# Moving the final products, a transposition and a copy inside a block of 32 passes

## The chip, the cores and the metric

One core of a Trainium2 chip runs the whole kernel in one launch. The metric is the device time of the launch in microseconds, the median of its runs. The work of this case lies on five engines of that core: TensorE (PE, the matrix products and transpositions), VectorE (DVE), ScalarE (ACT, the activation functions), GpSimd (POOL) and SyncE (SP, which issues the DMAs).

## What is computed

The input `x` (16 batches of 256 rows of 256) first passes a gated cross part (a long convolution over a context, two small networks) and then a gated mixture of experts; only the second half matters here. With `h = layernorm(x) @ Wm + bm` split into 8 heads of 32, so that there are 4096 x 8 small vectors `t`:

```python
logits = t @ expert_emb                       # 16 experts
w = softmax(logits); topw, topi = top_k(w, 2)
hmid = gelu(einsum('td,edi->tei', t, W1) + b1)    # every expert, 32 -> 128
eo = einsum('tei,eio->teo', hmid, W2) + b2        # 128 -> 32
comb = (eo at topi * topw).sum(over the two)
out = comb.reshape(rows, 256) @ Wo + bo
x = x + tanh(g_ffn) * out
```

The kernel computes all 16 experts for every vector and multiplies by a weight that is zero for the experts that were not chosen.

## The kernel before, in words

The 4096 rows are 8 blocks of 512 rows (b = 0 to 7). The first third of the launch (to about 303 us) is the cross part. Then comes the expert loop: `n` from 0 to 256, one pass for each of 8 blocks x 2 groups of four heads (g) x 16 experts (e), so a block is 32 passes. "Pass 5" below means n % 32 == 5. Every engine walks the same loop in its own program, and semaphores tie them.

- TensorE (lines 844 to 865), in each pass: `up(2n+2)` (line 780, eight fp16 products, 512 wide, each on a strip of 32 columns of the array), `down(n-1)` (line 792, four fp32 products, eight in the records), then `up(2n+3)`, eight products again. `up(k)` writes one of three pairs of PSUM banks (`pre`: PT, and two in PA) and so waits for the gelu three before it. `down` writes one of the two banks of PB in turn.
- ScalarE: `gelu(2n+2)`, `gelu(2n+3)` (line 1582), each 128 x 1024, out of the pair that `up` filled. At pass 26 of block 0 it computes three exponentials (line 1474), with a table load before and after.
- VectorE: `down(n-1)` (line 1333) multiplies the result by its weights and adds the bias, which frees the PB bank; then one of 14 steps of `route` (lines 1142 to 1183), which chooses the two experts of the next block, at the passes listed in `ROUTE`.
- GpSimd (line 1677) adds each product to the sum `AC[g]` of its 16 experts.
- After the 16th expert, VectorE's `down` ends with a copy of the sum to fp16 (line 1340, the high part; it waits for GpSimd's last addition), and GpSimd subtracts it from the sum for the low part (line 1681).
- Final products of a block, `finish` (line 814 on TensorE, 24 products in fp16, 256 wide; line 1376 on VectorE): one for each quarter of the block (t = 0 to 3), in the block that follows, at the passes in `FIN`, at the end of the pass. They too take a PB bank, and VectorE frees it.
- The turn of weights, `weights_turned` (line 692: four fp32 transpositions of 128 x 128; line 1368 on VectorE copies them out): once a block, for the next block, at the passes in `WT_AT`, ahead of the first `up` of the pass. SyncE stores the result in DRAM (`keep_weights`, line 447) and loads it back spread out (`spread_weights`, line 458: four DMAs for every two passes, four places `WB` in turn); `store` (line 463) writes results out.

PB's two banks go round over all uses in the order of TensorE's program (`output_uses`), turns, logits, `down` and final products alike: a use waits until VectorE has emptied the use two before it.

Of the kernel before, what the change touches and what calls it, by code (L numbers as in the profile page):

```python
# [13 lines left out]
NB = 8  # L14
# [11 lines left out]
N = 256  # L26
# [15 lines left out]
ROUTE = (1, 2, 3, 5, 6, 8, 9, 11, 13, 14, 15, 17, 19, 21)  # L42
ROUTE1 = (10, 11, 12, 13, 14, 15, 16, 17, 18, 19, 20, 21, 22, 23)

FIN = (4, 10, 22, 28)

WT_AT = {32 * b - 7: b for b in range(1, NB)}
LG_AT, EXP_AT = {8: 5, 12: 6, 24: 7}, 26

ROUTE0 = {4: range(0, 4), 5: range(4, 5), 6: range(5, 10), 7: range(10, 14)}  # L50
# [48 lines left out]
    return out  # L99


def output_uses():

    out = []
    for n in range(N + 1):
        if n in WT_AT:
            out.append(("wt", WT_AT[n]))
        if n in LG_AT:
            out.append(("lg", LG_AT[n]))
        if n >= 1:  # L110
            out.append(("down", n - 1))
        if n >= 32 and n % 32 in FIN:
            out.append(("fin", 4 * (n // 32 - 1) + FIN.index(n % 32)))
    return out


def flamingo_kernel(nc, xd, ctxT, peT, wp1, wp2, win, w1a, w1b, w2a, w2b, wm, wo,
                    ew1, ew2, eb, cols, rows, ident, ramp, tvec, ones, out):
    with ExitStack() as ctx:
# [4 lines left out]
        def sem(name):  # L124
            return ctx.enter_context(nc.semaphore(name))
# [63 lines left out]
        AC = [WK[:, 2048 + 512 * i:2048 + 512 * i + 512] for i in range(2)]  # L189
# [55 lines left out]
        def combined(b, g):  # L245

            return WM if b % 2 and not g else {h: CM[h][:, 512 * g:512 * g + 512] for h in "hl"}

        def iteration(n):
            return n // 32, n // 16 % 2, n % 16  # L250
# [17 lines left out]
        p_up, p_down, p_fin = (sem("p_" + n) for n in ("up", "down", "fin"))  # L268
# [15 lines left out]
        v_mul, v_cm, v_fin, v_wt = (sem("v_" + n) for n in ("mul", "cm", "fin", "wt"))  # L284
# [34 lines left out]
        def summed(n):  # L319

            b, g, e = iteration(n)
            return (g_ac, 15 * (n // 16) + e) if e else (v_mul, n + 1)
# [6 lines left out]
        def sync_program(sp):  # L329
# [130 lines left out]
            def store(b, u):  # L460
                sp.wait_ge(v_fin, 4 * b + 2 * u + 2)
                r0 = 512 * b + 256 * u
                sp.dma_start(out[r0:r0 + 256, :].rearrange("(t p) n -> p t n", p=128),
                             OB[u].rearrange("p (t n) -> p t n", t=2)).then_inc(s_out[u], 16)
# [7 lines left out]
            for n in range(0, N, 2):  # L472
                if n // 2 + 4 < N // 2:
                    spread_weights(n // 2 + 4)
                if n == 12:
                    spread_heads(7)
                if n % 32 == 22 and n // 32 + 1 < NB:
                    keep_weights(n // 32 + 1)
                if n >= 32 and n % 32 in (12, 30):
                    store(n // 32 - 1, n % 32 // 30)  # L480
            for u in range(2):
                store(NB - 1, u)
            for u in range(2):
# [4 lines left out]
        def tensor_program(pe):  # L488
# [319 lines left out]
            def finish(b, t):  # L808
                pf = take_po("fin", 4 * b + t)[:, 0:256]
                pe.wait_ge(g_cm, 2 * b + 2)  # L810
                for i, (g, (a, bb)) in enumerate((g, ab) for g in range(2) for ab in THREE):
                    for q in range(4):
                        r0 = 128 * t + 32 * q
                        m = pe.matmul(pf[32 * q:32 * q + 32, :], combined(b, g)[bb][:, r0:r0 + 32],  # L814
                                      WO[a][:, 256 * g:256 * g + 256], start=(i == 0), stop=(i == 5))
                m.then_inc(p_fin, 1)
# [29 lines left out]
            for n in range(N + 1):  # L846
                if n == HEADS6:
                    heads(6)
                    pe.wait_ge(v_out, 16)
                if n == TURN7:  # L850
                    third_turn(7)
                if n == HEADS7:
                    heads(7)
                if n in WT_AT:
                    weights_turned(WT_AT[n], take_po("wt", WT_AT[n]))
                if n in LG_AT:
                    logits(LG_AT[n], take_po("lg", LG_AT[n]))
                if n + 1 < N:
                    up(2 * n + 2)
                if 1 <= n < N:  # L860
                    down(n - 1)
                if n + 1 < N:
                    up(2 * n + 3)
                if n >= 32 and n % 32 in FIN:
                    finish(n // 32 - 1, FIN.index(n % 32))
            pe.wait_ge(g_cm, 2 * NB - 1)
            for t in range(2):
                last_products(0, t, range(3))
# [9 lines left out]
        def vector_program(ve):  # L878
# [443 lines left out]
            def down(n):  # L1322
                b, g, e = iteration(n)
                dst = PR[n % 3] if e else AC[g]
                ve.wait_ge(p_down, n + 1)
                if n % 2 == 0:
                    ve.wait_ge(l_wb[n // 2 % 4], 64 * (n // 8 + 1))
                if e == 0 and b:
                    ve.wait_ge(g_cm, 2 * (b - 1) + g + 1)
                elif e and n > 3:  # L1330
                    m = n - 3 if (n - 3) % 16 else n - 4
                    ve.wait_ge(*summed(m))
                ve.scalar_tensor_tensor(out=dst, in0=po("down", n), scalar=col(C_B2 + e),  # L1333
                                        in1=WB[n // 2 % 4][:, 512 * (n % 2):512 * (n % 2) + 512],
                                        op0=ALU.add, op1=ALU.mult).then_inc(v_mul, 1)
                if e == 15:
                    ve.wait_ge(*summed(n))
                    if b + g > 1:
                        ve.wait_ge(p_fin, 4 * (b + g - 1))
                    ve.tensor_copy(combined(b, g)["h"][:, :], AC[g]).then_inc(v_cm, 1)  # L1340

            def last_down(p):

# [26 lines left out]
            def finish(b, t):  # L1370
                u = t // 2
                ve.wait_ge(p_fin, 4 * b + t + 1)
                ve.wait_ge(g_xo, 4 * b + t + 1)
                if t % 2 == 0 and b:
                    ve.wait_ge(s_out[u], 16 * b)
                ve.scalar_tensor_tensor(
                    out=OB[u][:, 256 * (t % 2):256 * (t % 2) + 256], in0=po("fin", 4 * b + t)[:, 0:256] if b + 1 < NB else FL[t], scalar=GFS,
                    in1=XR[:, 1024 * b + 256 * t:1024 * b + 256 * t + 256], op0=ALU.mult, op1=ALU.add).then_inc(v_fin, 1)
# [5 lines left out]
            for n in range(N + 1):  # L1384
                if n == HEADS6 + 1:
                    heads_hi(6)
                    heads_lo(6)
                if n in NORM7:
                    last_norm(NORM7.index(n))
                if n == TURN7 + 1:  # L1390
                    turn_hi(turn3(7))
                    turn_lo(turn3(7))
                if n == HEADS7 + 1:
                    heads_hi(7)
                    heads_lo(7)
                if n in WT_AT:
                    weights(WT_AT[n], po("wt", WT_AT[n]))
                if n in LG_AT:
                    less_max(LG_AT[n], po("lg", LG_AT[n]))
                if 1 <= n < N:  # L1400
                    down(n - 1)
                when = ROUTE if n >= 32 else ROUTE1
                if n // 32 + 1 < NB and n % 32 in when:
                    route(n // 32 + 1, when.index(n % 32))
                if n >= 32 and n % 32 in FIN:
                    finish(n // 32 - 1, FIN.index(n % 32))
            for p in range(2):
                last_down(p)
            for t in range(4):
# [189 lines left out]
        def pool_program(po_):  # L1599
# [57 lines left out]
            for n in range(N + 1):  # L1657
                if n == 2:
                    po_.wait_ge(l_bo, 16)
                    po_.wait_ge(a_tanh, 1)  # L1660
                    po_.tensor_scalar(RB[:, :], RB[:, :], GF, None, ALU.mult).then_inc(g_bo, 1)
                if n < N and n % 32 in (14, 18, 22, 26):
                    b, t = n // 32, (n % 32 - 14) // 4
                    if n == 14:
                        po_.wait_ge(g_bo, 1)
                        po_.wait_ge(a_n3, 7)
                    add_row(XR[:, 1024 * b + 256 * t:1024 * b + 256 * t + 256]).then_inc(g_xo, 1)
                if n >= 1:
                    m = n - 1
                    b, g, e = iteration(m)  # L1670
                    if m == N - 2:
                        break
                    if e:
                        po_.wait_ge(v_mul, m + 1)
                        if e > 1:
                            po_.wait_ge(*summed(m - 1))
                        po_.tensor_tensor(AC[g], AC[g], PR[m % 3], ALU.add).then_inc(g_ac, 1)  # L1677
                    if e == 15:
                        hi, lo = (combined(b, g)[h][:, :] for h in "hl")
                        po_.wait_ge(v_cm, 2 * b + g + 1)  # L1680
                        po_.tensor_tensor(lo, AC[g], hi, ALU.subtract).then_inc(g_cm, 1)
# [81 lines left out]
```

## Time and profile before

| | us |
|---|---|
| time, median of 3 runs | 810.44 |
| the runs | 810.2, 813.04, 810.44 |
| profiled execution: first to last instruction (its span) | 807.5 |
| PE busy | 774.8 (96%) |
| ACT busy | 670.3 (83%) |
| DVE busy | 531.4 (66%) |
| POOL busy | 496.0 (61%) |
| first gelu of the loop starts | 303.4 |
| granted TensorE clock, mean | 0.986 |

The profiled execution is given by its span alone; the time of a launch has a little more around it (the median of the runs is 2.9 us above the span). Engine times overlap, so they do not add up to the span. In the loop both TensorE and ScalarE are nearly always at work, so that what counts is which of the two makes the other wait, and where.

### The profile page before, as it was taken

The numbers are of one execution on the slowest core, as the hardware profiler recorded it, in microseconds if no ns is written. First come the engines' busy times: TensorE is split into PE (matmuls) and PEld (weight loads), VectorE is DVE, ScalarE is ACT, GpSimd is POOL, SyncE is SP. The second block draws the span as 40 slices with busy tenths as digits, with TensorE's granted clock in tenths as the row PEclk, the third lists the DMA queues.
The fourth block names the chain that finished last, engine by engine and source line by source line (L and its number), as shares of the span: only waits on it lengthen the run. The fifth ranks groups of instructions, "written<-read, shape, count | busy, mean of one in ns | idle before, by whom it ended". The sixth has DMA issues, their size and how long they took to land.

```text
span 807.5 us, 23892 instructions
## 1 busy us (share of the span) xinstructions
PE 774.8 (96%) x9972; PEld 380.7 (47%) x9972; DVE 531.4 (66%) x988; ACT 670.3 (83%) x840; POOL 496.0 (61%) x389
## 2 busy tenths in 40 slices
PE   9999788889999998998999999999999999999997
PEld 4667455646676664333334434434434433434433
DVE  5999854557688985684665664764764764664445
ACT  4465854445869878799999999999999999999995
POOL 1374332027753542585787787787787787787674
PEclk9999999979999999999999999999999999999999
DMA  8990699941133316655465554555555555465552
GB/s 291 219 244 28 135 187 191 198 107 36 50 86 89 89 44 166 156 143 149 145 158 151 166 157 147 159 170 146 157 159 151 165 159 155 148 171 158 149 154 67
DMA packets 85971, 117.06 MB, mean 145 GB/s; under 512 B 13123, under 2 KB 65475, under 8 KB 85764
## 3 DMA queue, kind: packets, MB, share of 16 engines
q1 hardware_dynamic: 85864, 115.55, 55.2%
q8 instruction: 78, 1.28, 0.7%
q14 instruction: 29, 0.24, 0.1%
HBM read 101.28 MB, written 6.94 MB: 134 GB/s over the span
## 4 chain that ended last, share of the span: by engine, by line
PE 71%; DVE 10%; ACT 7%; SPq 5%; issue 3%; DMA 2%; POOL 2%; POOLq 0%; DVEq 0%; ACTq 0%
PE PB L792 26%; PE PA L780 18%; PE PT L780 9%; PE PA L581 5%; SPq L345 4%; PE PB L598 3%; PE PB L814 2%; PE PA L535 2%; DMA RA<-wpd 2%; DVE WK L897 2%; DVE SM L914 1%; ACT WK L1458 1%; PE PT L673 1%; ACT WK L1438 1%; ACT WK L1435 1%
## 5 line engine op out<-in xcount | busy, mean ns | idle before, releaser
L1677 POOL TENSOR_TENSOR WK<-WK 128x512 f32<-128x512 f32 x238 | 320.3, 1346 | 112.3 <-DVE WK L1333 102.2
L1582 ACT ACTIVATE WK<-PA 128x1024 f32<-128x1024 f32 x349 | 360.1, 1140 | 10.8 <-PE PA L780 10.3
L792 PE MATMUL PB<-WK,EW 128*32 128x512 f32 x2040 | 264.7, 594 | 0.4 <-DVE WK L1333 0.4
L780 PE MATMUL PA<-RA,EW 98*32 98x512 f16 x2800 | 201.6, 380 | 0.5 <-ACT WK L1582 0.5
L1582 ACT ACTIVATE WK<-PT 128x1024 f32<-128x1024 f32 x163 | 187.1, 1148 | 2.0 <-PE PT L780 1.7
L1610 POOL TENSOR_TENSOR WK<-WK 128x512 f16<-128x512 f32 x64 | 79.5, 1255 | 129.9 <-ACT WK L1438 128.6
L780 PEld LDWEIGHTS PA<-RA,EW 98*32 98x32 f16 x2800 | 68.1, 95 | 154.9 <-issue 80.4
L780 PE MATMUL PT<-RA,EW 98*32 98x512 f16 (+1 forms) x1312 | 99.6, 379 | 4.8 <-ACT WK L1582 3.4
L792 PEld LDWEIGHTS PB<-WK,EW 128*32 128x32 f32 x2040 | 62.4, 111 | 52.3 <-DVE WK L1333 0.9
L1333 DVE SCALAR_TENSOR_TENSOR WK<-PB,CV,W2h 128x512 f32<-128x512 f32 x64 | 48.1, 751 | 49.1 <-PE PB L792 49.1
L1333 DVE SCALAR_TENSOR_TENSOR WK<-PB,CV,W2l 128x512 f32<-128x512 f32 x63 | 47.3, 751 | 44.3 <-PE PB L792 44.3
L1333 DVE SCALAR_TENSOR_TENSOR WK<-PB,CV,DC 128x512 f32<-128x512 f32 x64 | 47.8, 748 | 37.1 <-PE PB L792 36.7
L780 PEld LDWEIGHTS PT<-RA,EW 98*32 98x32 f16 x1312 | 32.5, 95 | 76.9 <-issue 35.7
L1333 DVE SCALAR_TENSOR_TENSOR WK<-PB,CV,W1h 128x512 f32<-128x512 f32 x64 | 47.7, 746 | 29.0 <-PE PB L792 29.0
L1435 ACT ACTIVATE WK<-PA,CV 128x512 f16<-128x512 f32 x64 | 44.1, 690 | 24.6 <-PE PA L581 23.9
L1604 POOL TENSOR_TENSOR SM<-SM 128x4 f32<-128x4 f32 (+1 forms) x24 | 33.2, 1385 | 40.5 <-DVE SM L927 22.5
L1438 ACT ACTIVATE WK<-PA,CV 128x512 f32<-128x512 f32 x64 | 44.2, 690 | 0.0
L598 PE MATMUL PB<-W1h,WK 128*128 128x256 f16 x256 | 42.5, 273 | 1.0 <-issue 1.0
L598 PE MATMUL PB<-W2h,WK 128*128 128x256 f16 x256 | 42.5, 273 | 0.9 <-POOL WK L1610 0.9
L581 PE MATMUL PA<-WK,W1h 128*128 128x512 f16 x128 | 38.7, 384 | 0.0
L581 PE MATMUL PA<-WK,W2h 128*128 128x512 f16 x128 | 38.1, 379 | 0.0
L1080 DVE TENSOR_REDUCE DC<-PB 128x256 f32<-128x512 f32 x28 | 19.2, 691 | 26.6 <-PE PB L638 26.6
(220 smaller groups left out, 1086.8 us busy)
## 6 DMA issues: line engine op xcount, KB each, us to landing
RA<-wpd SPq DMA_DIRECT2D x128, 134.1 KB, 5.8
W1h<-wtd SPq DMA_DIRECT2D x128, 128.0 KB, 2.7
DC<-wtd SPq DMA_DIRECT2D x128, 128.0 KB, 2.8
W2h<-wtd SPq DMA_DIRECT2D x128, 128.0 KB, 2.7
W2l<-wtd SPq DMA_DIRECT2D x128, 128.0 KB, 2.7
WK<-in_x SPq DMA_DIRECT2D x15, 512.0 KB, 4.0
RA<-DC SPq DMA_DIRECT2D x96, 64.0 KB, 2.0
out<-WK SPq DMA_DIRECT2D x16, 256.0 KB, 2.8
```

What stands on the lines that cost most here:

```text
L345: sp.dma_start(slot(c)[p0:p0 + K1, :, :, :].rearrange("p q i n -> p (q i) n"), src).then_inc(l_T[c % TR], 16)
L581: m = pe.matmul(pa, w[a][:, 512 * k + 128 * n:512 * k + 128 * n + 128], xt[b][:, 512 * k:512 * k + 512], start=(i == 0), stop=(i == 5))
L598: m = pe.matmul(o[t], S[b][:, 512 * k + 128 * t:512 * k + 128 * t + 128], w[a][:, 1024 + 256 * k:1024 + 256 * k + 256], start=False, stop= ...
L780: m = pe.matmul(pre(k)[32 * j:32 * j + 32, w * q:w * q + w], EW1[0:98, 128 * e + 32 * j:128 * e + 32 * j + 32], TS[0:98, h, t0:t0 + w], st ...
L792: m = pe.matmul(o[32 * q:32 * q + 32, :], EW2[:, 32 * e:32 * e + 32], hb[:, 512 * q:512 * q + 512], start=True, stop=True)
L1333: ve.scalar_tensor_tensor(out=dst, in0=po("down", n), scalar=col(C_B2 + e), in1=WB[n // 2 % 4][:, 512 * (n % 2):512 * (n % 2) + 512], op0= ...
L1435: ac.activation(S["h"][:, 512 * n:512 * n + 512], pa, ACT.Silu, scale=1.0 / SC, bias=col(bcol + n))
L1438: ac.activation(SF[n], pa, ACT.Silu, scale=1.0 / SC, bias=col(bcol + n)).then_inc(a_silu, 1)
L1582: ac.activation(HB[n % NH][:, 1024 * p:1024 * p + 1024], pre(k)[:, :], ACT.Gelu, scale=1.0 / (SC * SC)).then_inc(a_gelu, 1)
L1604: po_.tensor_tensor(SM[:, o:o + n], SM[:, o:o + n], SM[:, 6:7].broadcast_to([128, n]), ALU.pow).then_inc(g_pow, 1)
L1610: po_.tensor_tensor(sl, SF[n], sh, ALU.subtract).then_inc(g_slo, 1)
L1677: po_.tensor_tensor(AC[g], AC[g], PR[m % 3], ALU.add).then_inc(g_ac, 1)
```

## The change

Four edits, all in the expert loop:

1. The final products move from passes 4, 10, 22, 28 to 5, 11, 19, 31. In the last block (n from 224 on) they stay at 4, 10, 22, 28.
2. The turn of weights moves from pass 25 to pass 26 (in block 0 as well).
3. SyncE's second store of a block moves from its pass 30 to its pass 0 of the block after (for the last-but-one block: behind the loop).
4. The copy of the high part (line 1340) goes behind the `down` that follows it, that of the next group's first expert; GpSimd's subtraction moves likewise by one pass of its own.

```diff
-FIN = (4, 10, 22, 28)
-
-WT_AT = {32 * b - 7: b for b in range(1, NB)}
+FIN, FIN_LAST = (5, 11, 19, 31), (4, 10, 22, 28)
+
+WT_AT = {32 * b - 6: b for b in range(1, NB)}
...
+def fin_at(n):
+
+    f = FIN if n < 32 * (NB - 1) else FIN_LAST
+    return (n // 32 - 1, f.index(n % 32)) if n >= 32 and n % 32 in f and n < N else None
...
-                if n >= 32 and n % 32 in (12, 30):
-                    store(n // 32 - 1, n % 32 // 30)
+                if n >= 64 and n % 32 == 0:
+                    store(n // 32 - 2, 1)
+                if n >= 32 and n % 32 == 12:
+                    store(n // 32 - 1, 0)
+            store(NB - 2, 1)
...
-                if n >= 32 and n % 32 in FIN:
-                    finish(n // 32 - 1, FIN.index(n % 32))
+                if fin_at(n):
+                    finish(*fin_at(n))
...
-                if e == 15:
-                    ve.wait_ge(*summed(n))
-                    if b + g > 1:
-                        ve.wait_ge(p_fin, 4 * (b + g - 1))
-                    ve.tensor_copy(combined(b, g)["h"][:, :], AC[g]).then_inc(v_cm, 1)
+                if n and e == 0:
+                    combined_hi(n - 1)
+
+            def combined_hi(n):
+
+                b, g, e = iteration(n)
+                ve.wait_ge(*summed(n))
+                if b + g > 1:
+                    ve.wait_ge(p_fin, 4 * (b + g - 1))
+                ve.tensor_copy(combined(b, g)["h"][:, :], AC[g]).then_inc(v_cm, 1)
...
-                    if e == 15:
+                    elif m:
+                        b, g, e = iteration(m - 1)
                         hi, lo = (combined(b, g)[h][:, :] for h in "hl")
                         po_.wait_ge(v_cm, 2 * b + g + 1)
                         po_.tensor_tensor(lo, AC[g], hi, ALU.subtract).then_inc(g_cm, 1)
```

(`fin_at` replaces the test with `FIN` on TensorE, on VectorE and in `output_uses`.)

## Rows read from the trace of the kernel before

**Rows 1.** Windows, block 3: us, busy PE PEld DVE ACT POOL, PEclk, DMA share, GB/s.
```profile
502.78:562.07 59.29, 59.29 (x872) 24.18 (x868) 36.79 (x53) 58.90 (x65) 46.46 (x37) 1.00 0.52 157
```
**Rows 2.** Timeline of ACT (start, us, what), block 3: two gelus, 18 apart.
```profile
527.50 1.07 ACT L1582 ACTIVATE WK<-PT 128x1024 f32<-128x1024 f32 x1
...
543.76 1.31 ACT L1582 ACTIVATE WK<-PT 128x1024 f32<-128x1024 f32 x1
```
**Rows 3.** Timeline of PE: final product of pass 10, first `up` of passes 11 and 16.
```profile
523.04 0.41 PE L814 MATMUL PB<-WOh,WK 128*32 128x256 f16 x8
...
523.70 0.62 PE L780 MATMUL PT<-RA,EW 98*32 98x512 f16 x8
...
532.33 0.64 PE L780 MATMUL PA<-RA,EW 98*32 98x512 f16 x8
```
**Rows 4.** Timeline of PE: the turn of weights at pass 25, block 3.
```profile
548.71 0.60 PE L780 MATMUL PT<-RA,EW 98*32 98x512 f16 x8
549.24 0.66 PE L692 MATMUL PB<-ID,WK 128*128 128x128 f32 x4
549.83 0.62 PE L780 MATMUL PA<-RA,EW 98*32 98x512 f16 x8
```
**Rows 5.** Timeline of ACT: gelus behind passes 10, 22 and 25.
```profile
524.60 1.22 ACT L1582 ACTIVATE WK<-PT 128x1024 f32<-128x1024 f32 x1
525.68 1.98 ACT L1582 ACTIVATE WK<-PA 128x1024 f32<-128x1024 f32 x2
...
546.47 1.35 ACT L1582 ACTIVATE WK<-PT 128x1024 f32<-128x1024 f32 x1
547.64 2.02 ACT L1582 ACTIVATE WK<-PA 128x1024 f32<-128x1024 f32 x2
...
551.79 1.03 ACT L1582 ACTIVATE WK<-PA 128x1024 f32<-128x1024 f32 x1 [0.27 <-PE PA L780]
```
**Rows 6.** Timeline of PE: two `up` with a wait for ACT between them, pass 18.
```profile
535.43 1.14 PE L780 MATMUL PA<-RA,EW 98*32 98x512 f16 x16
536.40 1.03 PE L792 MATMUL PB<-WK,EW 128*32 128x512 f32 x8
```
**Rows 7.** Timeline of all engines: turn of weights in block 0, and what follows.
```profile
365.99 0.60 PE L780 MATMUL PT<-RA,EW 98*32 98x512 f16 x8
366.65 1.02 ACT L1582 ACTIVATE WK<-PT 128x1024 f32<-128x1024 f32 x1
...
367.31 0.62 PE L780 MATMUL PA<-RA,EW 98*32 98x512 f16 x8
...
368.62 0.61 PE L780 MATMUL PA<-RA,EW 98*32 98x512 f16 x8
...
369.27 1.03 ACT L1582 ACTIVATE WK<-PA 128x1024 f32<-128x1024 f32 x1 [0.27 <-PE PA L780]
...
375.67 1.05 PE L780 MATMUL PT<-RA,EW 98*32 98x512 f16 x8 [3.43 <-ACT WK L1582]
```
**Rows 8.** Windows behind the exponentials.
```profile
375.50:378.90 3.40, 3.23 (x24) 0.80 (x28) 0.00 (x0) 3.40 (x5) 0.00 (x0) 0.52 0.10 31
```
**Rows 9.** The page's fifth part: weight loads of `down`, and whom they waited for.
```profile
L792 PEld LDWEIGHTS PB<-WK,EW 128*32 128x32 f32 x2040 | 62.4, 111 | 52.3 <-DVE WK L1333 0.9
```
**Rows 10.** Timeline of DVE: two route steps, and the copy at pass 16.
```profile
529.40 0.68 DVE L1166 TENSOR_TENSOR W1l<-W1l,RMP 128x512 f32<-128x512 f32 x1
...
536.56 0.43 DVE L1340 CAST WMh<-WK 128x512 f16<-128x512 f32 x1 [1.89 <-POOL WK L1677]
...
540.02 1.33 DVE L1178 TENSOR_TENSOR W1l<-W1l 128x512 f32<-128x512 f32 x1
```
**Rows 11.** Timeline of SP and DVE, and the page's sixth part: next block's weights.
```profile
554.44 1.70 SPq L458 DMA_DIRECT2D W1h<-wtd  x4
...
566.60 0.74 DVE L1333 SCALAR_TENSOR_TENSOR WK<-PB,CV,W1h 128x512 f32<-128x512 f32 x1
...
W1h<-wtd SPq DMA_DIRECT2D x128, 128.0 KB, 2.7
```

More of the change, by code:

```diff
@@ L111, in output_uses @@
             out.append(("down", n - 1))
-        if n >= 32 and n % 32 in FIN:
-            out.append(("fin", 4 * (n // 32 - 1) + FIN.index(n % 32)))
+        if fin_at(n):
+            out.append(("fin", 4 * fin_at(n)[0] + fin_at(n)[1]))
     return out
@@ L863, in tensor_program @@
                     up(2 * n + 3)
-                if n >= 32 and n % 32 in FIN:
-                    finish(n // 32 - 1, FIN.index(n % 32))
+                if fin_at(n):
+                    finish(*fin_at(n))
             pe.wait_ge(g_cm, 2 * NB - 1)
@@ L1404, in vector_program @@
                     route(n // 32 + 1, when.index(n % 32))
-                if n >= 32 and n % 32 in FIN:
-                    finish(n // 32 - 1, FIN.index(n % 32))
+                if fin_at(n):
+                    finish(*fin_at(n))
             for p in range(2):
```

## Prediction

> **What bounds the kernel now.** I read four views in this order. The windows first: in a block of the loop (32 passes, 59.29 us) the trace has TensorE at work all the time and ScalarE for 58.90 us of it [rows 1], so the two take turns as the bound and no share of busy time says which. The timelines of the two tell it. ScalarE unhindered starts 18 gelus in 543.76 - 527.50 = 16.26 us, 0.903 us each, 1.807 us for the two of a pass [rows 2]; 32 passes are 57.81 us. TensorE unhindered goes through five passes in 532.33 - 523.70 = 8.63 us, 1.726 us each [rows 3]; 32 passes are 55.23 us. A final product puts 523.70 - 523.04 = 0.66 us on top (0.655 over several) [rows 3]; the turn of weights 549.83 - 548.71 = 1.12 us less the 0.43 us of the eight `up` products ahead of it, 0.69 us [rows 4]. With four and one of them TensorE's work in a block is 55.23 + 2.62 + 0.69 = 58.54 us. That is more than ScalarE's 57.81, and less than the 59.30 that a block takes. So TensorE is the bound by work, and in each block it stands idle for 59.30 - 58.54 = 0.76 us; ScalarE loses 59.30 - 57.81 = 1.49 us to it.
>
> Where the 0.76 us are: TensorE gains 1.807 - 1.726 = 0.081 us a pass on ScalarE, until it is three pairs of banks ahead and has to wait for a gelu. After a final product has used up its lead it can gain for six passes; from the seventh it waits, as at pass 18, where the two `up` last 536.40 - 535.43 = 0.97 us instead of 0.86 [rows 6]. In the twelve passes between 10 and 22 it waits so at 17 to 22, six times some 0.10 us; at the four or less from 22 to 25 to 28 it cannot gain what the next extra costs, and ScalarE pays.
>
> As a check, the rule "an extra delays ScalarE by its length less 0.081 us for each pass since the last one, plus what TensorE idled in them" against the gelus behind the extras: pass 10 (six passes after 4) gives 0.655 - 0.484 = 0.17 us, and the gelu comes 1.08 us after the one before it, 0.18 too late [rows 5]. Pass 25, two full passes after 22, gives 0.69 - 0.16 = 0.53; the four gelus from 547.64 to 551.79 take 4.15 us instead of 3.61, 0.54 too long [rows 5]. Pass 22, with its twelve passes and 0.60 idle: 0.655 - 0.97 + 0.60 = 0.29, seen 546.47 to 547.64, 1.17, 0.27 too late [rows 5].
>
> **Edits 1 and 2, the distances.** The extras stand at 5, 11, 19, 26 and 31 of blocks 1 to 6. The same count of instructions, so TensorE's 58.54 us stay, and the gain is idle time alone. Pass 31 to 5, 5 to 11: six passes each, 0.17 us each for ScalarE. 11 to 19: eight passes, 0.655 - 0.645 plus one or two waits at 18 and 19, 0.10 to 0.19 us [rows 6]: 0.11 to 0.20, I take 0.165. 19 to 26: the turn stands ahead of its pass, so six full passes, 0.69 - 0.484 = 0.21. 26 to 31: six passes again, 0.17. Sum 3 x 0.17 + 0.165 + 0.21 = 0.88; the block takes 57.81 + 0.88 = 58.69 us, 0.61 less than before. Bounds of this: 0.76 (no idle left) and, where TensorE still idles at three places, about 0.4. Blocks 2 to 6: 5 x 0.61 = 3.05 us. Block 1 begins with no final product at the end of block 0, and its first is at 5 rather than 4: seven passes, 0.11 instead of 0.17, so 0.68 us. Block 7 has the old passes, but its first extra now comes five passes after one at 31 and not eight after one at 28: 0.655 - 0.40 = 0.25 against 0.14 before, a loss of 0.11. Together 3.62 us.
>
> **Edit 2 in block 0.** Here the turn at pass 25 lies straight ahead of ScalarE's exponentials, with ScalarE already short of work. The `up` after it begins at 367.31; without turn (and without its wait for a bank) it would follow the one of 365.99 after 0.43, at 366.42. The next one, 368.62 - 367.31 = 1.31 later, comes at 367.73, its gelu 0.65 us behind that [rows 7] at 368.38, or after the two gelus from 366.65 at 0.903 each, 368.46. It is at 369.27 before, so the exponentials start 0.81 us earlier. The turn itself then runs while ScalarE computes them, when TensorE idles 3.43 us [rows 7] anyway, now some 3.0; that idle time hides it, and without it the 0.69 us would come back. I take 0.80, bounds 0.4 and 0.9. Behind the idle time TensorE runs at a granted clock of 0.52 for 3.4 us (the lower level, 1.2 of 2.4 GHz) [rows 8], a cost of up to 0.8 us in gelus that come late. Whether 3.0 us of idleness instead of 3.4 still lead to it no row tells; I leave it in, and if it goes, the time is up to 0.8 less.
>
> **Edit 3.** The store of the second half waits for the final product at 31, which VectorE has consumed when SyncE comes to it, since the four DMAs ahead of it wait for `down` of pass 1. It is one issue on SP, ahead of `spread_weights` of pass 2. The turn one pass later delays the load of the next block's first weights by 1.8 us: issued from 554.44 on, 1.70 us long and 2.7 to landing, it is there at 558.8 and first used at 566.60, a margin of 7.8 us [rows 11]. Cost 0; between 0 and, if the margin were gone, 0.1 a block.
>
> **Edit 4.** The copy makes VectorE wait for GpSimd's last addition, 1.89 us at pass 16 [rows 10], with a finished `down` behind it. Behind that `down` the wait mostly vanishes. But who waits for VectorE? TensorE's `down` waited for it 0.9 us in the whole launch [rows 9]: PB's second bank covers the delay. So the 15 copies bring between 0 and 0.9 us, and I take 0. In the other direction, the next thing behind the copy on VectorE is a route step or a `down`, and GpSimd's subtraction comes no later than before where the addition is what the copy waits for; the first final product needs its low part four passes later. Below nothing too: up to 0.43 us (the copy) late at a bank, twice a block, if the cover failed.
>
> Here a rule of the Trainium skill speaks against the change. The same route work of 128 x 512 takes 0.68 us at 529.40 and 1.33 us at 540.02, where GpSimd adds beside it [rows 10]. "SBUF — State Buffer", section "Who interferes with whom", says that a VectorE instruction with two inputs in SBUF contends with a GpSimd instruction that reads SBUF, and that the one to start later blocks. By it, shifting the copy reshuffles these pairs; final products at 5, 11 and 19 now stand behind a route step on VectorE, which they never did. The sum stays as it is; the rule's outcome is the second rival.
>
> **Sum.** 3.62 + 0.80 = 4.4 us off the profiled execution: span 807.5 to 803.1. The median of the runs is 2.9 above that span; nothing around the loop changes, so I take the same from it: 810.44 - 4.4 = 806.0 us.
>
> **Rivals.**
> 1. The lead is not what holds TensorE: the new distances move idle time about and a block saves 0.2 or less (the two waits between 11 and 19 become three, and one more ahead of 31). For it: the old 28 to 4, eight passes, held an idle 0.10 us. Against: the rule above meets three gelus to 0.02. 6 x 0.2 + 0.8 = 2.0, 808.4 us.
> 2. Slower: VectorE gives banks back late. At pass 19 `route` takes 1.33 us [rows 10] and the final product's bank is freed only behind it. It is needed by the second `down` after, which in the trace of before leaves some 0.8 us. If VectorE is as late as the 1.89 us that it waited at the copy [rows 10], TensorE waits 1.1 us at pass 19, and at pass 5 behind the copy of pass 1 the same: 2 x 1.1 x 6 = 13.2 - 4.4 = 8.8 us more, 819.2. It decides from 0.8 us of lateness. Against: VectorE is at work 36.79 of 59.29 us [rows 1], and it is the wait for GpSimd that edit 4 removes.
> 3. All goes well: no idle left (0.76 x 6 = 4.6 + 0.07 in block 1 - 0.1), and the clock stays up behind a shorter idle time (0.5): 4.5 + 0.8 + 0.5 = 5.8, 804.6 us.
> 4. The change doesn't do what it says: the turn in block 0 waits at pass 26 for something else and gives nothing; only the distances count: 3.6, 806.8 us.
>
> **How the numbers follow.** Forecast 0.55, rival 1 0.17, rival 2 0.05, rival 3 0.13, rival 4 0.10. Half a per cent is 4.05 us, about what a measurement can tell from no change. The forecast lies just beyond it: with the bounds of its terms (0.4 to 0.76 a block, 0.4 to 0.9 in block 0) three quarters of it are past 4.05, rival 3 wholly, a third of rival 4 by chance of the runs: 0.41 + 0.13 + 0.03 = 0.57 faster. Slower is rival 2, 0.05; the rest, 0.38, is within. The range reaches from rival 3 to rival 1, 804.6 to 808.4.
>
> **What would show it.** Right: blocks 2 to 6 of 58.7 us from first gelu to first gelu; TensorE's two adjacent `up` always 0.86 us apart but at passes 18 and 19; gelus late by 0.17 to 0.21 behind each of the five extras; the exponentials 0.8 us earlier; the copy with hardly a wait, and the same 0.9 us of `down` waiting for VectorE. Wrong: blocks above 59, weight loads of `down` or final products waiting for DVE, a final product waiting for GpSimd's subtraction, or a block 0 that ends as late as before.

## The result, and the profile after

| | before | changed |
|---|---|---|
| median of 6 runs each, us | 810.32 (807.21 to 813.04) | 803.11 (800.8 to 805.38) |
| ratio | | 0.992 (95%: 0.9893 to 0.9948) |
| the profiled execution: time | | 805.38 |
| its span, us | 807.5 | 803.6 |
| span before the loop's first gelu | 303.40 | 303.31 |
| block 0 | 80.76 | 80.34 |
| block 1 | 59.32 | 58.59 |
| blocks 2 to 6 | 59.30 to 59.31 | 58.69 to 58.72 |
| block 7 to its last gelu's start | 57.69 | 57.96 |
| behind it | 9.84 | 9.84 |

A block is counted from the start of its first gelu to that of the next block's first, and a pass likewise, so that pass 26 of block 0 holds the exponentials. The kernel is faster by 0.8%, the interval reaches from 0.5 to 1.1%. Forecast were 806.0 us and 804.6 to 808.4: the sign was right and the profiled execution moved by 3.9 us where 4.4 were said, but the measured median lies below the range. One later launch of before took 1137.83 us at a mean granted clock of 0.65 and is left out of every ratio.

Line numbers shift with the edits: in the changed kernel `up` is line 789, `down` 801, the final product 823, VectorE's `down` 1342, its copy of the high part 1354, the gelu 1596 and GpSimd's addition 1691; in the kernels of the experiments they differ by a few.

The page after: busy times, and the line of its fifth part that answers to [rows 9].

```profile
PE 770.5 (96%) x9972; PEld 396.9 (49%) x9972; DVE 524.4 (65%) x988; ACT 668.9 (83%) x840; POOL 499.3 (62%) x389
...
L801 PEld LDWEIGHTS PB<-WK,EW 128*32 128x32 f32 x2040 | 66.8, 111 | 47.9 <-DVE WK L1342 0.9
```

TensorE loads the same weights, and its `down` still waits 0.9 us for VectorE in all, but the idle time ahead of those loads fell from 52.3 to 47.9 us. The 0.9 us is one wait in block 0; in two more launches of the same kernel the waits of `down` for VectorE are 3.3 us, all in block 0 too. The copy of the high part, [rows 10], waited 23.8 us for GpSimd in its 15 times before, and now

```profile
  POOL WK L1691: 1.0, 6
```

1.0 us in 6 of them. The windows, block 3 and the stretch behind the exponentials, against [rows 1] and [rows 8]:

```profile
500.94:559.66 58.72, 58.72 (x873) 27.09 (x868) 35.70 (x53) 58.72 (x65) 46.98 (x37) 1.00 0.53 159
375.50:378.90 3.40, 3.21 (x27) 0.95 (x29) 0.37 (x1) 2.89 (x4) 0.00 (x0) 0.53 0.23 55
```

Now ScalarE is busy in the whole block (58.72 of 58.72; before 58.90 of 59.29). TensorE around the final product of pass 19, its first `up` of pass 18 and what is left of the idle time, against [rows 3] and [rows 6]:

```profile
533.81 1.08 PE L789 MATMUL PA<-RA,EW 98*32 98x512 f16 x16
534.72 1.04 PE L801 MATMUL PB<-WK,EW 128*32 128x512 f32 x8
535.58 0.61 PE L789 MATMUL PT<-RA,EW 98*32 98x512 f16 x8
536.11 0.61 PE L789 MATMUL PA<-RA,EW 98*32 98x512 f16 x8
...
537.41 0.61 PE L789 MATMUL PA<-RA,EW 98*32 98x512 f16 x8
537.85 0.39 PE L823 MATMUL PB<-WOh,WK 128*32 128x256 f16 x8
```

The two `up` at 533.81 take 0.91 us and the one at 535.58 is followed after 0.53, where 0.86 and 0.43 are the times without a wait, so 0.05 and 0.10 us idle, ahead of passes 18 and 19 as forecast; with them TensorE's 58.54 us of work are 58.69. The gelus behind pass 5, 11 and the turn, against [rows 5]:

```profile
512.87 2.05 ACT L1596 ACTIVATE WK<-PA 128x1024 f32<-128x1024 f32 x2
514.85 1.02 ACT L1596 ACTIVATE WK<-PT 128x1024 f32<-128x1024 f32 x1
...
523.90 2.06 ACT L1596 ACTIVATE WK<-PA 128x1024 f32<-128x1024 f32 x2
525.87 1.02 ACT L1596 ACTIVATE WK<-PT 128x1024 f32<-128x1024 f32 x1
...
550.41 1.23 ACT L1596 ACTIVATE WK<-PT 128x1024 f32<-128x1024 f32 x1
551.51 1.96 ACT L1596 ACTIVATE WK<-PA 128x1024 f32<-128x1024 f32 x2
```

From 512.87 to 514.85 are two gelus and 1.98 us, 0.17 more than 1.81; behind pass 11 it is 1.97, behind the turn 1.10 for one (0.20 more): the 0.17 and 0.21 of the forecast. The prediction did not read a gelu's own duration, which is 1.02 behind each delay and grows from there, to 1.23 at 550.41; it is the subject of the fifth experiment.

### The profile page after: what moved, and what is told of

Read it like the earlier page. It is cut to its first block, busy times and chain, and to the rows that moved or that the text cites. A ratio compares the mean times of both kernels' runs of the same rounds, so it can differ in the third digit from the quotient of the medians.

```text
span 803.6 us, 23892 instructions
## 1 busy us (share of the span) xinstructions
PE 770.5 (96%) x9972; PEld 396.9 (49%) x9972; DVE 524.4 (65%) x988; ACT 668.9 (83%) x840; POOL 499.3 (62%) x389
## 4 chain that ended last, share of the span: by engine, by line
PE 68%; DVE 10%; ACT 8%; DMA 5%; SPq 4%; issue 3%; POOL 1%; POOLq 0%; DVEq 0%; ACTq 0%
PE PB L801 27%; PE PA L789 18%; PE PT L789 9%; SPq L351 4%; PE PA L590 3%; PE PB L607 3%; DMA RA<-wpd 3%; PE PB L823 2%; DVE WK L906 2%; DVE SM L923 1%; DMA WK<-in_eb 1%; ACT WK L1472 1%; PE PT L682 1%; ACT WK L1452 1%; ACT WK L1596 1%
## 5 line engine op out<-in xcount | busy, mean ns | idle before, releaser
L1596 ACT ACTIVATE WK<-PA 128x1024 f32<-128x1024 f32 x349 | 354.2, 1109 | 9.1 <-PE PA L789 9.1
L1596 ACT ACTIVATE WK<-PT 128x1024 f32<-128x1024 f32 x163 | 181.7, 1115 | 1.2 <-PE PT L789 1.1
L789 PEld LDWEIGHTS PA<-RA,EW 98*32 98x32 f16 x2800 | 75.7, 96 | 145.6 <-issue 83.1
L801 PEld LDWEIGHTS PB<-WK,EW 128*32 128x32 f32 x2040 | 66.8, 111 | 47.9 <-DVE WK L1342 0.9
L1342 DVE SCALAR_TENSOR_TENSOR WK<-PB,CV,W2l 128x512 f32<-128x512 f32 x63 | 47.3, 750 | 44.3 <-PE PB L801 44.3
L789 PEld LDWEIGHTS PT<-RA,EW 98*32 98x32 f16 x1312 | 36.2, 96 | 71.5 <-issue 38.2
```

The lines of the kernel that those rows point to most:

```text
L789: m = pe.matmul(pre(k)[32 * j:32 * j + 32, w * q:w * q + w], EW1[0:98, 128 * e + 32 * j:128 * e + 32 * j + 32], TS[0:98, h, t0:t0 + w], st ...
L801: m = pe.matmul(o[32 * q:32 * q + 32, :], EW2[:, 32 * e:32 * e + 32], hb[:, 512 * q:512 * q + 512], start=True, stop=True)
L1596: ac.activation(HB[n % NH][:, 1024 * p:1024 * p + 1024], pre(k)[:, :], ACT.Gelu, scale=1.0 / (SC * SC)).then_inc(a_gelu, 1)
```

## The experiments

A ratio is always to launches of the kernel before made beside it on the same chip, with its 95% interval.

**1. The changed kernel again, twice (`again`, `again2`), and the kernel before against itself (`before_again`).** No edit.

> The changed kernel unaltered, timed again. The profiled executions differ by 3.9 us (span 807.5 to 803.6), the medians by 7.2. Theory A (launches of one kernel scatter by several us, and the loop's blocks hold the whole change): ratio to before near 0.9952 (3.9 of 810.4), at most 0.993; blocks 2 to 6 again 58.7 us, and whatever this profile's span differs from 803.6 by lies outside the blocks. Theory B (something outside the blocks became faster too): ratio again 0.991 to 0.992, and a stretch outside blocks 1 to 6 that is shorter by 2 us or more.

> The changed kernel unaltered, a third time. Theory A (launches scatter ahead of the loop by up to 6 us, the change itself is the 3.6 us of the blocks and 0.3 to 0.7 of block 0): ratio to before 0.9945 to 0.9952. Theory B (the first measurement's 0.992 was the true one): 0.992 or less.

> The kernel before, run as a candidate against itself. Ratio 1.000 within 0.0025; blocks 1 to 6 of 59.30 us and a tail of 9.84 us whatever the span, with start of the loop between 298 and 305 us and block 0 between 79 and 82 us taking all of the scatter.

| | runs | median | ratio | span | to first gelu | block 0 | block 1 | blocks 2 to 6 | block 7 | tail |
|---|---|---|---|---|---|---|---|---|---|---|
| again | 11 | 804.12 | 0.9942 (0.992 to 0.9965) | 802.49 | 302.50 | 80.09 | 58.57 | 58.69 to 58.72 | 57.96 | 9.85 |
| again2 | 9 | 804.66 | 0.9947 (0.9924 to 0.997) | 802.10 | 301.33 | 80.97 | 58.57 | 58.68 to 58.69 | 57.96 | 9.85 |
| before_again | 12 | 808.97 | 0.9999 (0.9977 to 1.0021) | 807.25 | 303.14 | 80.76 | 59.32 | 59.30 | 57.69 | 9.84 |

The 0.9952 of theory A and the forecast's 0.9946 (806.0 of 810.44) lie in both intervals; theory B's 0.992 is the very edge of the one and outside the other. The stretch it needs was not found: the start of the loop lies 0.1, 0.9 and 2.1 us earlier in the three traces of the changed kernel than in the first of before, but in other kernels it moves by more, with the same instructions ahead of it. From launch to launch of the one kernel blocks 1 to 7 and the tail repeat to 0.04 us. The start of the loop does not: over all eleven traces of this case it lies between 298.63 and 304.44 us; and block 0 takes 79.2 to 81.7. The two traces of before have the same 80.76 for block 0, the three of the changed kernel 80.09 to 80.97. Three runs of before gave 810.44 as their median, where 20 and 34 runs of it gave 809.33 and 809.17.

**2. The copy alone (`only_copy`).**

```diff
-                if e == 15:
-                    ve.wait_ge(*summed(n))
...
+                if n and e == 0:
+                    combined_hi(n - 1)
```

> The kernel before with edit 4 alone: the copy of the high part behind the next down, GpSimd's subtraction likewise. Prediction's theory: TensorE waits for VectorE only 0.9 us in all, so blocks stay at 59.30 us and the time within 1 us of before. Rival: the copy's wait is worth the 2 to 3 us that the forecast missed, time 807.5 to 808.5.

Ratio 1.0002 (0.9978 to 1.0025), 12 runs, median 808.10; blocks 1 to 6 of 59.30 each. The median is 1.07 us below that of before beside it, and inside the rival's 807.5 to 808.5, but the ratio sees no difference and the blocks did not move. The copy by itself brings nothing that can be seen, as forecast, and can't be the missing microseconds.

**3. The places alone (`only_places`).** The changed kernel with that copy, and GpSimd's subtraction, put back.

```diff
-                if n and e == 0:
-                    combined_hi(n - 1)
+                if e == 15:
+                    ve.wait_ge(*summed(n))
...
```

> The changed kernel with edit 4 undone: final products, turn of weights and store moved, the copy where it was. Prediction's theory: all of the change, blocks 58.7 us, block 0 80.3, time equal to that of the changed kernel within 1 us. Rival (VectorE late at the banks of passes 5 and 19 without edit 4): blocks of 59 us or more, and weight loads of down that wait for DVE.

Ratio 0.9954 (0.9932 to 0.9976), 12 runs, median 805.95. Blocks 2 to 6 take 58.79 to 58.82, 0.1 more each than in the changed kernel. The median is 1.8 us above the changed kernel's 804.12, not the 1 us or less that was expected, but the intervals of the two ratios overlap by most of their length; and block 0 takes 81.58 and not 80.3, in a launch with a longer stretch of low clock (experiment 6). The timeline of all engines at passes 17 to 19 says where:

```profile
531.64 0.43 DVE L1349 CAST WMh<-WK 128x512 f16<-128x512 f32 x1 [1.88 <-POOL WK L1686]
531.99 0.74 DVE L1342 SCALAR_TENSOR_TENSOR WK<-PB,CV,W1h 128x512 f32<-128x512 f32 x1
...
532.65 1.22 DVE L1184 TENSOR_TENSOR W1l<-W1l,SM 128x512 f32<-128x512 f32 x1
...
533.79 0.74 DVE L1342 SCALAR_TENSOR_TENSOR WK<-PB,CV,W1h 128x512 f32<-128x512 f32 x1
...
534.06 0.60 PE L789 MATMUL PA<-RA,EW 98*32 98x512 f16 x8
...
534.58 0.12 PEld L823 LDWEIGHTS PB<-WOh,WK 128*32 128x32 f16 x8 [0.41 <-DVE WK L1342]
```

VectorE waits 1.88 us for GpSimd's addition before the copy, is late with the `down` at 531.99 and, behind a route step of 1.22 us, with the one at 533.79; the final product of pass 19 needs the bank that this one frees at 534.53, and starts at 534.58, where the `up` of 534.06 would let it start 0.43 behind, at 534.49. In the waits of this kernel it is one row, absent in the changed kernel's:

```profile
PEld PB L823 <- DVE WK L1342: 2.4, 6, 0.4
```

The six times are pass 19 of blocks 1 to 6. So the prediction's second rival was real in small: its place (pass 19, VectorE late behind the copy and a route step) is right, its price 0.1 us a block and not 1.1, and edit 4 is what removes it. At pass 5, where that rival saw the same, no wait is found. The copy is worth 0.6 us in the profile once the places are moved (blocks 2 to 6 with 0.10 to 0.13 each, block 7 with 0.03), and nothing before. The gain of the blocks is thus in edits 1 to 3, and by experiment 4 not in edit 2; the store of edit 3 was never run apart from the final products of edit 1, so that its part, forecast at 0, is argued and not shown.

**4. The turn at pass 26 alone (`turn26`).**

```diff
-WT_AT = {32 * b - 7: b for b in range(1, NB)}
+WT_AT = {32 * b - 6: b for b in range(1, NB)}
```

> The kernel before with the turn of weights at pass 26 instead of 25, nothing else. By the forecast's rule: blocks 1 to 6 unchanged (59.3), since TensorE's idle time between 10 and 22 stays; block 0 shorter by 0.4 us, as in the changed kernel's profile (exponentials 0.9 earlier, 0.4 given back at pass 29 under the low clock), rather than the 0.8 forecast. Time 0.4 us less than before. Rival: distances 22-26-28 help as well, blocks 59.1 or less.

Ratio 0.9983 (0.9961 to 1.0006), 12 runs, median 807.94. Blocks 1 to 6 are 59.30 to 59.33: nothing but block 0 moves, whose passes 25 and 26 take 2.21 and 6.23 us instead of 2.62 and 6.62, and in this launch its pass 29 takes 2.31, as before. So the exponentials come 0.8 us earlier, and pass 29 need not give it back. Block 0 as a whole is 79.16, 1.6 us less than before and not the 0.4 expected; the other 0.8 lie ahead of its pass 24, a part which takes 59.26 us here and 59.65 to 60.17 in the other ten traces, whatever the kernel, and can't be put down to the edit. The rival's blocks of 59.1 did not come.

**5. What ScalarE's own pace is (`short_fin`).** The changed kernel with one of six sets of products left in each final product of the loop.

```diff
-                for i, (g, (a, bb)) in enumerate((g, ab) for g in range(2) for ab in THREE):
+                for i, (g, (a, bb)) in enumerate(((0, THREE[0]),)):
```

> The changed kernel with five sixths of each final product of blocks 1 to 7's passes left out on TensorE (4 products instead of 24, so 0.11 us instead of 0.655; the outputs of blocks 0 to 6 are not the reference's). TensorE's work in a block falls by 4 x 0.545 = 2.2 us to 56.4. Prediction's theory: ScalarE's own pace is the 0.903 us between starts, so the block falls to 57.8 us. Rival, read from the ends of the gelus, which are 0.917 us apart while each grows by 0.013 us: that is ScalarE's real pace, 64 x 0.917 = 58.7, and the block stays at 58.7 us, as in the changed kernel.

One run, 802.3 us. Its window of block 3, and gelus of it:

```profile
500.50:559.17 58.67, 58.67 (x796) 19.63 (x788) 35.53 (x54) 58.67 (x66) 46.86 (x37) 1.00 0.53 158
```

```profile
509.31 1.31 ACT L1596 ACTIVATE WK<-PT 128x1024 f32<-128x1024 f32 x1
...
522.87 1.50 ACT L1596 ACTIVATE WK<-PT 128x1024 f32<-128x1024 f32 x1
...
533.72 1.65 ACT L1596 ACTIVATE WK<-PT 128x1024 f32<-128x1024 f32 x1
534.63 2.56 ACT L1596 ACTIVATE WK<-PA 128x1024 f32<-128x1024 f32 x2
536.47 1.65 ACT L1596 ACTIVATE WK<-PT 128x1024 f32<-128x1024 f32 x1
```

The waits of TensorE's weight loads for a gelu, of this kernel and then of the changed one:

```profile
PEld PA L789 <- ACT WK L1596: 101.8, 284, 0.8
```

```profile
PEld PA L789 <- ACT WK L1596: 44.3, 134, 0.8
```

Blocks 2 to 6 take 58.67 us each although 2.2 us of TensorE's work in each are gone. The prediction's theory wanted 57.8 and falls; the rival's 58.7 is met. What TensorE was spared it spends waiting for gelus, 101.8 us instead of 44.3 at these loads, while ScalarE is never idle in the window. The rows show how the starts deceive: from 509.31 to 522.87 fifteen gelus start 0.904 us apart while one's duration grows from 1.31 to 1.50, so their ends are 0.917 apart; at 1.65 the growth stops, and from 533.72 to 536.47 three take 2.75, 0.917 each in the starts too. The same is in [rows 2]: the two gelus end at 528.57 and 545.07, 16.50 us for 18.

**6. The low clock behind the exponentials (`warm`).** 11 products on TensorE in the idle time at pass 27 of block 0.

```diff
+                if n == 27:
+                    bank = take_po("warm", 0)
+                    for _ in range(11):
+                        m = pe.matmul(bank, ON[:, 0:128], ON[:, :], start=True, stop=True)
+                    m.then_inc(p_warm, 1)
```

> The changed kernel with 11 idle products (128 x 512 of ones, 2.4 us) on TensorE at pass 27 of block 0, between a down and the up that waits for the exponentials, into a free bank. Theory (the low clock behind the idle time delays the gelus of passes 29 and 30, which gave back 0.4 us of edit 2's gain): no low stretch near 370 to 378 us, passes 29 and 30 of 1.81 us, 0.5 to 1.1 us off block 0. Rival (the delay comes from the exponentials' wait itself or from the order of the banks): passes 29 and 30 as long as in the changed kernel, 2.7 and 1.8 or 2.3 and 2.4 us.

Ratio 0.9947 (0.9922 to 0.9972), 12 runs, median 803.44 beside 808.39 of before. The timeline of TensorE, and a window:

```profile
372.54 2.55 PE L876 MATMUL PB<-ON 128*128 128x512 f16 x11
375.44 0.62 PE L791 MATMUL PT<-RA,EW 98*32 98x512 f16 x8 [0.35 <-ACT WK L1603]
```

```profile
376.50:379.90 3.40, 3.40 (x48) 1.02 (x40) 0.91 (x2) 3.40 (x5) 1.16 (x1) 1.00 0.10 23
```

The clock stays at 1.00 (2.4 GHz), where the changed kernel has 0.53 behind an idle time of 2.83 us, and passes 29 and 30 take 1.81 us each. Block 0 is 79.45 us; the changed kernel's, in a launch with the same first passes, 80.34. So the low clock costs 0.9 us there. The page "TensorE: Matmul & The Clock Gate" of the Trainium skill, section "What's actually happening", has it that the throttled state is the default and activity releases it; the traces agree in so far as the two kernels with products in this idle time (this one and the next) have no low stretch behind it, and all nine other traces, idle for 2.83 or 3.43 us, have one. In the time of launches 0.9 us are too little to be seen.

The 0.9 us is the price in one launch. The low stretch stands at another place in other launches of the same kernel, and is longer in some. In `again` TensorE takes up its work at 373.57 us and the clock falls at 375.2; in `again2` it does so at 372.43, inside a stretch that began at 371.7:

```profile
375.20:378.60 3.40, 3.40 (x28) 1.08 (x24) 0.75 (x1) 3.08 (x5) 1.10 (x1) 0.50 0.10 18
371.80:378.50 6.70, 6.08 (x48) 1.72 (x52) 0.75 (x1) 5.74 (x7) 1.27 (x1) 0.50 0.31 95
```

Against 3.62 us for passes 29 and 30 together, `again` loses 1.0 us and `again2` 1.9; the two traces of before and `turn26` lose 0.5, `only_places` 2.1.

**7. Even distances everywhere (`warm_spread`).** The same, and

```diff
-FIN, FIN_LAST = (5, 11, 19, 31), (4, 10, 22, 28)
+FIN, FIN_LAST = (5, 11, 18, 31), (6, 13, 20, 27)
```

> The same with final products at 5, 11, 18, 31 (last block 6, 13, 20, 27), so that no distance is over 7 passes. By the pace of starts (0.903) TensorE never idles: blocks 58.54 us, the last 57.3 instead of 57.96, time 1.7 us under that of the other kernel. By the pace of ends (0.917) blocks stay at 58.67 to 58.70, and the last block is 57.5 to 57.8.

Ratio 0.9943 (0.9917 to 0.997), 9 runs, median 803.52. Blocks 2 to 6 are 58.68 to 58.70 and block 7 is 57.78 instead of 57.96: the pace of ends again, and 0.2 us in all. The pace of starts wanted 58.54 and 57.3, and falls a second time. It beats the kernel before; against `warm` and the changed kernel no difference can be measured.

## Why the prediction was right, and where it failed

**The blocks: right in number.** 58.69 us were forecast for blocks 2 to 6 and 58.69 to 58.72 came; 0.61 a block, 3.05 in five, measured 2.99. Block 1: 0.68 forecast, 0.73 measured.

**The blocks: wrong in cause.** "ScalarE unhindered ... 0.903 us each; 32 passes are 57.81 us. So TensorE is the bound by work" was read from starts. Experiment 5 shows 0.917 us a gelu, 58.67 a block. TensorE's 58.54 us of work lie just under that, and the changed kernel's 58.70 is ScalarE's floor plus 0.03. The prediction's own rows held the contradiction: at 0.081 us a pass TensorE regains only 0.49 of the 0.655 of a final product in six passes, and yet it waited from the seventh on. From the ends it gains 1.833 - 1.726 = 0.107 us a pass, and six passes regain 0.64. The rule of the delays gave the right numbers because it was calibrated on starts: behind a delay the starts catch up while the durations grow, and the "0.17 us behind each extra" is mostly that debt coming due, not time lost. So the 58.69 is a hit by calibration, not by the cause that was given. The rule would have promised 0.9 us a block to whoever took more work off TensorE, where 0.03 are to be had.

**Block 7: a loss of 0.11 forecast, 0.27 measured.** The delay behind the final product at 31 of block 6 (pass 1 of block 7, 0.18) belonged to the next block's account. From end to end of gelus the loss is 57.91 - 57.75 = 0.16 us.

**Block 0: 0.80 forecast, 0.42 measured in this pair of traces.** What the forecast worked out came: passes 25 and 26 together are 0.8 us shorter in every trace with the turn at 26, and the table load ahead of the exponentials starts at 369.43 instead of 370.32 us, 0.89 earlier, of which 0.09 is the earlier start of the loop. TensorE, whose timeline has against [rows 7]

```profile
374.78 0.61 PE L789 MATMUL PT<-RA,EW 98*32 98x512 f16 x8 [2.83 <-ACT WK L1596]
```

takes up its work as much earlier, but pass 29 takes 2.71 us instead of 2.31. The term that failed is the cost "behind the idle time TensorE runs at a granted clock of 0.52": the text had it as something fixed that might vanish, not as one that might grow. In this pair the low stretch began at 375.4 and at 375.3 us and lasted 3.4 both times, so that it came 0.3 us before TensorE took up its work in the one and 0.5 behind that in the other. That they agree is chance: over the nine traces that have it, the stretch begins between 369.6 and 375.4 us, from 1.2 us before TensorE takes up its work to 1.7 behind, it lasts 3.4 or 6.8 us, and its cost is 0.5 to 2.1 us (experiment 6). A fixed cost was the wrong form of this term, and no pair of traces can tell block 0's gain to better than that.

**Edit 4: 0 forecast.** Right alone (experiment 2), wrong in company: with the final product at 19, it saves 0.1 us a block (experiment 3).

**Edit 3 and the rule on VectorE and GpSimd: 0, and no such loss.** Blocks of 58.70 us over a floor of 58.67 leave no room for either. The reading that led to the rule needs a correction: GpSimd adds beside both of the route steps of [rows 10]. The one at 529.40 began first and took 0.68 us, and then it was GpSimd's addition that was long:

```profile
529.56 1.67 POOL L1677 TENSOR_TENSOR WK<-WK 128x512 f32<-128x512 f32 x1 [0.44 <-DVE WK L1333]
```

1.67 us instead of 1.29 for the one before it. At 540.02 GpSimd was already adding, and the route step took 1.33. The one to start later is the one that is held up, which is the rule that the prediction cites.

**The range: this is what failed.** The step is the last of the sum: "The median of the runs is 2.9 above that span; nothing around the loop changes, so I take the same from it: 810.44 - 4.4 = 806.0". It took 2.9 us for a fixed difference and a median of three runs for the kernel's time, and the range held only the bounds of the terms of the loop. In the runs on record the time of a launch is 1.8 us above its own span (1.7 to 2.5); the rest of the 2.9 was scatter between the profiled launch and the others. After the change the median, 803.11, is 0.5 us below the profiled span of 803.6.

Single runs of before lie between 803.6 and 815.1 us in the later measurements, and of the changed kernel between 800.8 and 807.0. All 91 runs of before together have a median of 809.0 us and all 26 of the changed kernel one of 804.2, so of the 2.9 us between 806.0 and 803.11 some 1.4 are the 810.44 that the sum began with, 1.1 are the first six runs of the changed kernel, and 0.4 are left for the change itself. Even 804.2 lies just below the range, for the first of these reasons. Against the 4.4 forecast the first six runs of each gave 7.2 by the medians, and 6.5 by the ratio (0.8% of 810); two more measurements of the same kernel give 4.7 and 4.3 by the ratio (0.58% and 0.53% of 809). The profiles give 3.9. The forecast's 0.9946 is inside all three intervals; what it said of the median was too sharp.

What makes the start of the loop vary by 6 us was located and not explained. The eleven traces are within 1.1 us of each other at 60 us of the launch and 5.7 apart at 178, in the cross part; from there to the loop the distance stays. Stretches of low clock lie there, at other places in each trace, but their summed length does not account for it: the same 13.6 us of them stand ahead of a loop that starts at 303.40 us (before) and at 298.63 (`only_places`). No experiment was made on it, and the cause stays open.

## What to carry to other kernels

An engine's own pace is the distance between the ends of its instructions, or between starts only once their durations stand still; growing durations at even starts are a queue that fills, not speed to spare. Where two engines are bound within 1% of each other, short pieces on the one cost nearly nothing if they stand at least as far apart as its lead takes to recover, here six or seven passes (0.655 / 0.107 and 0.69 / 0.107, an estimate from the rows above); find that lead in the rows and count the distances. And before a range of half a per cent is given, compare the launches of the one kernel with each other: a stretch that repeats to 0.03 us may sit behind one that scatters by 6.

## What was not expected of the hardware

The low clock behind one and the same idle time of TensorE (2.83 us, six traces) does not come at a fixed distance from it: it began from 0.7 us before TensorE took up its work to 1.7 behind, and lasted 3.4 or 6.8 us. And on ScalarE two successive activations of 128 x 1024 overlap in the records by up to 0.73 us (durations of 1.65 at 0.917 apart), 0.1 when it had been waiting.
